# A graph network kernel: in the last message round ScalarE takes a tile's sums first, and two small transfers are issued later in the step

## The reference

```python
def step(h, Wl):                      # five rounds, h is 6250 x 256
    m = h @ Wl
    agg = segment_sum(m[src], dst)    # the neighbours' rows, summed by node
    gi = agg @ w_ih.T + b_ih
    gh = h @ w_hh.T + b_hh
    ...
    r = sigmoid(ir + hr); z = sigmoid(iz + hz)
    ng = tanh(in_ + r * hn)
    return (1 - z) * ng + z * h
...
y = relu(concat([h, x]) @ l0_w.T + l0_b)
y = relu(y @ l1_w.T + l1_b)
```

## Time and profile before

| | us |
|---|---|
| median of 3 runs | 9063.8 (9062.63 to 9071.94) |
| the profiled execution's own time | 9073.26 |
| its span in the trace | 9071.5 |
| PE busy | 6295.3 (69%) |
| POOL busy | 6524.4 (72%) |
| DVE busy | 5542.8 (61%) |
| ACT busy | 2574.8 (28%) |

### The profile page before, as it was taken

One profiled execution on the slowest core, in us unless ns is written; L12 is line 12 of the kernel. 1 busy time (PEld: TensorE's weight loads), 2 busy tenths in 40 slices (PEclk: granted clock), 3 DMA queues, 4 the chain that ended last, 5 costly groups with the idle time before them and its releaser, 6 DMA issues. The chain is left out here.

```text
span 9071.5 us, 161491 instructions
## 1 busy us (share of the span) xinstructions
PE 6295.3 (69%) x36545; PEld 5409.3 (60%) x36546; DVE 5542.8 (61%) x13908; ACT 2574.8 (28%) x6581; POOL 6524.4 (72%) x7005
## 2 busy tenths in 40 slices
PE   0011255552444498888888888888888999889998
PEld 0000133332333377777777677767776888778887
DVE  9999444442444466656665566656664666556666
ACT  4223111112333211121112111111112333456665
POOL 1777777777777777767777677767776777657776
PEclk9755566665555599999999999999999999989999
DMA  4000222222222244434443444444443444212223
GB/s 153 7 7 18 58 79 77 78 68 61 59 59 59 80 143 137 138 103 143 137 138 108 137 139 136 129 117 138 138 138 104 135 124 127 71 53 63 64 64 53
DMA packets 428100, 870.71 MB, mean 96 GB/s; under 512 B 117433, under 2 KB 229680, under 8 KB 427349
## 3 DMA queue, kind: packets, MB, share of 16 engines
q0 software_dynamic: 269952, 615.62, 25.2%
q10 hardware_dynamic: 122250, 189.76, 6.2%
q1 hardware_dynamic: 35529, 61.49, 2.1%
HBM read 763.02 MB, written 103.40 MB: 96 GB/s over the span
## 5 line engine op out<-in xcount | busy, mean ns | idle before, releaser
L1027 POOL DMA_INDIRECT rows<-state_table,rec x3440 | 3290.6, 957 | 1185.9 <-issue 1105.8
L1100 PE MATMUL l_prod<-rows,onehot 128*125 x10728 | 2640.3, 399 | 1210.6 <-SPq L1041 523.8
L1141 DVE TENSOR_TENSOR agg<-agg,l_prod 125x256 f32 (+2 forms) x5364 | 2038.7, 380 | 2185.2 <-PE l_prod L1100 1156.2
L1100 PEld LDWEIGHTS l_prod<-rows,onehot 128*125 128x125 f32 x10728 | 2010.8, 223 | 1637.4 <-issue 1440.4
L2313 POOL DMA_INDIRECT w_area<-xcol_table,l_slots x832 | 787.7, 947 | 346.6 <-issue 250.4
L1027 POOL DMA_INDIRECT rows<-rel_table,rec x782 | 740.4, 947 | 255.5 <-issue 238.2
L1027 POOL DMA_INDIRECT rows<-in_x_dram,rec x782 | 740.8, 947 | 251.2 <-issue 232.0
L1837 PE MATMUL l_prod<-l_sources,rec 125*125 125x256 f32 x3000 | 695.1, 382 | 24.6 <-DMA rec<-dense_table 23.9
L474 POOL DMA_INDIRECT slots_table<-rec_stage,row_stage x528 | 553.1, 1048 | 161.6 <-issue 143.2
L1837 PEld LDWEIGHTS l_prod<-l_sources,rec 125*125 125x125 f32 x3000 | 562.9, 189 | 118.2 <-DMA rec<-dense_table 30.8
L1792 PE MATMUL l_rh<-state,w_area 128*128 x4000 | 591.0, 282 | 3.0 <-DVE l_u L2121 3.0
(11 more groups left out here) (427 smaller groups left out, 10314.1 us busy)
## 6 DMA issues: line engine op xcount, KB each, us to landing
rec<-dense_table ACTq DMA_DIRECT2D x125, 732.4 KB
rows<-state_table,rec POOLq DMA_INDIRECT x3440
l_sources<-state_table ACTq DMA_DIRECT2D x125, 250.0 KB
rel_table<-l_relrow ACTq DMA_DIRECT2D x50, 500.0 KB
state_table<-l_row ACTq DMA_DIRECT2D x200, 125.0 KB
dense_table<-late_rec SPq DMA_DIRECT2D x50, 366.2 KB
w_area<-xcol_table,l_slots POOLq DMA_INDIRECT x832
rows<-in_x_dram,rec POOLq DMA_INDIRECT x782, 2.5
```

Of the source, the lines that this page charges most:

```text
L1027: pool.indirect_dma_start(out=K["rows"][:, r, 0:width], out_offset=None, in_=table, in_offset=bass.IndirectOffsetOnAxis(ap=K["rec"][:, wor ...
L1100: last = pe.matmul(slots[k][0:LANES, 0:width], K["onehot"][:, h % ONEHOTS, k, :], rows[:, bass.ds(at[k], width)], start=True, stop=True)
L1141: dve.tensor_tensor(into, into, of, ALU.add).then_inc(S.added, 1)
```

## The change

Three things move in `last_body`, all on ACT. The load of x, with its wait and register load, goes from ahead of `take` to the end of part n = 1. The store of the projected columns goes from the end of its own step's n = 3 to n = 1 of the next step (so it names `turn.has(b, 3)` and the other buffer). `take` thereby comes first.

```diff
                     load_next(turn, b, LAST)
                     for n in range(4):
                         if n == 0 and now is not None:
-                            if turn.has(b, 2):
-                                act.wait_ge(y_step, turn.place_in_round(b, 2) * 2 + 2)
-                            tile = numbers_of(nc, act, ACTE, K["slot_tile1"], turn.place_in_round(b), 1, TILES - 1)[0]
-                            act.dma_start(xs[:, odd, :], x2_rows[:, bass.ds(tile, 1), :].rearrange("p t f -> p (t f)"))\
-                                .then_inc(xs_in[odd], 16)
                             take(turn, b, now)
...
                             last.then_inc(hid_ok, 1)
+                        if n == 1 and now is not None:
+                            if turn.has(b, 2):
+                                act.wait_ge(y_step, turn.place_in_round(b, 2) * 2 + 2)
+                            tile = numbers_of(nc, act, ACTE, K["slot_tile1"], turn.place_in_round(b), 1, TILES - 1)[0]
+                            act.dma_start(xs[:, odd, :], x2_rows[:, bass.ds(tile, 1), :].rearrange("p t f -> p (t f)"))\
+                                .then_inc(xs_in[odd], 16)
+                        if n == 1 and turn.has(b, 3):
+                            place = turn.place_in_round(b, 3)
+                            tile = numbers_of(nc, act, ACTE, K["slot_tile1"], place, 1, TILES - 1)[0]
+                            act.wait_ge(proj_ok, place + 1)
+                            act.dma_start(col_rows[:, bass.ds(tile, 1), :].rearrange("p t f -> p (t f)"),
+                                          colrow[:, 1 - odd, :]).then_inc(col_out[1 - odd], 16)
...
                             act.copy(K["agg"][0:LANES, bass.ds(old, D)], proj_ps[0:LANES, 0, :]).then_inc(proj_ok, 1)
-                            act.wait_ge(proj_ok, place + 1)
-                            act.dma_start(col_rows[:, bass.ds(tile, 1), :].rearrange("p t f -> p (t f)"),
-                                          colrow[:, odd, :]).then_inc(col_out[odd], 16)
```

More of the change, by code:

```diff
@@ L2072, in last_body @@
                             old = numbers_of(nc, act, ACTE, K["slot_col1"], place, 1, (TILES - 1) * SLOT)[0]
-                            tile = numbers_of(nc, act, ACTE, K["slot_tile1"], place, 1, TILES - 1)[0]
                             act.wait_ge(proj_ps_ok, place + 1)
```

## The result

The changed kernel takes 8968.6 us (8965.9 to 8976.5, 4 runs), the kernel before 9063.2 (9055.8 to 9071.9, 4 runs): a ratio of 0.9899 [0.9886, 0.9912], 94.7 us less. The forecast was 52.5 us less, 9011 us, and its range ended at 8998. The sign was right, and the size a little over half of what came.

A forecast was written before the change was run, and what follows sets the result against it. In the last message round PE was taken to set the pace, waiting for ACT's `take`. Terms of 22.5 + 18 + 12 = 52.5 us gave 9011 us from the median 9063.8, range 8998 to 9036 us.

The forecast's parts named there:

- first part: Last message round: PE sets the pace, waiting 22.5 us for ACT's `take`, once in each of 20 b = 0 steps.
- what is late next: Chunk sum of n = 1 (L1100), behind L1852: moves up with it; 0.2 us a turn, 4 us, left to the range.
- don't hold it: Chunk sum of n = 1: DVE's dense additions end at 7783.30, before PE would come to it at 7784.51.
- Term 1: b = 0 steps of the last round: PE's wait for `take` goes whole, 22.5 us.
- Term 2: Windows from b = 0 to b = 1: eight slow-clock windows recover once PE's wait goes, 18 us, lower bound nothing.
- the gathers become the bound: Turns of the last round: POOL's ring empties in places, half of 40 us is lost, 9031 us; chance 0.10.
- Term 3: Six tail steps: ACT reaches `take` sooner after the last copy, 2.0 of 2.78 us each; 12 us, bounds 9.5 and 15.
- the rival with 0.12: Tail: the clock comes back there too, 7 us more, 9004 us; chance 0.12.
- What it adds: Mid-step on ACT, ahead of gate z: two issues and two loads, 1.9 us, covered by waiting, so costing nothing.
- the sign that it named: ACT's wait before gate z shrinks to about 2 us in the steps and under 1 in the tail, but stays.
- The figure of 50 ns: DMA dispatch time; by it two issues free 0.1 us of ACT, not 1.04, and the tail gives about 6 us.
- x load too late: L1916 of the next step: x landing after about 12.8 us makes a loss, 9126 us at 14 us; chance 0.03.

The follow-up runs named there:

- before_pe_loads_2: Kernel before, ACT untouched; only PE's register loads for the n = 1 chunk sums moved ahead of its wait for `take`: 9004.1 us, ratio 0.9940.
- store_only_2: Kernel before with only the store of the projected columns moved to n = 1 of the next step: 9021.7 us, ratio 0.9953.
- The single edits: Kernel before with only the load of x moved (8998.0 us), and with only the store of the projected columns moved (9021.7 us).
- after_busy_tail: Changed kernel with PE's n = 1 register loads ahead of its wait for `take`, product h_b repeated twice more in the last three turns: 8979.8 us, ratio 0.9900.

## Why the prediction was half of it

**The sentence that failed** is in its first part: "PE waits for `take` at no b = 1 step before the tail", taken from "PE starts L1852 with no idle time in front of it". The engine was not idle, but its sequence was held until `take` ended (7806.42), and the register loads that the next sum needs came only then. The same step closed the question of "what is late next": the pause behind L1852 was said to follow PE's register loads, "and moves up with L1852", at a gain of 0.2 us in 20 steps. It shrank by 0.6 us at b = 0 and 0.8 at b = 1, 25.7 us in all, for which the sum had nothing. What "moves up" is not tied to L1852 but to the end of `take`. before_pe_loads_2 shows this cause by itself. DVE's additions, which "don't hold it" in the prediction, do hold the sum at b = 1 once the loads are out of the way, for 0.47 us.

**Term 1, 22.5 us:** right, the wait is gone. **Term 2, 18 us of clock:** the clock is back at 1.00 throughout the turns, and PE's busy time fell by 17.0 us. The reason given (PE's idling) is shown for the tail. In the turns the reason is incomplete, and that the size came out is partly luck: removing the pause alone does it too, and store_only_2, whose waits are shorter, loses the clock in more windows.

The parts of the turns now add up: 22.5 + 25.7 + 17.0 = 65 us against 63.9. The single edits sum to more than the whole (57.7 + 13.9 = 71.6); both shorten the same wait, so by itself this shows no other bound. The rival "the gathers become the bound" fits: POOL's wait for freed chunks fell from 50.8 us to 2.7 (about 10 were forecast), and 15 of its writes of slots moved from the turns into the tail (35 to 20; the gathers are 581 in both). It took nothing from what was forecast. That POOL is the floor at 765 to 772 us is argued, not shown by a run of its own. For it speaks that four kernels end there whose PE idles between 19 and 36 us; against it, that PE is itself busy 739.9 of the 764.8 us and is put down as waiting for rows for only 1.5.

**Term 3, the tail:** mis-sized, 12 for 23.4. The remaining register load was counted with 0.7 us behind the copy; it costs nothing, since it runs under the table load, and 2.8 us a step go (5.0 to 2.2, 17 in six steps), above even the bound of 2.5. The rest, 6.4 us, is the clock, and the repeated products give the same (11.2 - 4.8): the rival with 0.12 came true in size, 6.4 us where it had 7, with three of the six steps at 1.00.

**What it adds** was right at nothing, and the cover that it counted on (ACT's wait for gate z) was there. Only the sign that it named was wrong: it saw this wait shrink to 2 us and under 1. It did not move, for it is idle time of ACT's engine, and the issues run in ACT's sequence meanwhile. The figure of 50 ns that the prediction takes from the Trainium skill (DMA: Bandwidth & Descriptors, section "Anatomy of one DMA — SWDGE (gpsimd) path") is for DMAs that POOL issues, by the section's own title. ACT's 0.51 and 0.53 us neither confirm nor contradict it. **x load too late:** no. L1916 follows L1852 in every step with no idle time.

**What is the best version?** No kernel tried is measurably faster than the changed one. after_busy_tail has the shortest tail, 4.8 us less, and the same ratio in whole time (0.9900 against 0.9899).

## What to carry to other kernels

Read two timelines for each engine: its work, and its sequence of register loads, waits and issues. If a load or an issue behind a wait feeds the next instruction, the lateness of what is waited for is paid even where the engine shows no idle time; the pause then stands one instruction further on, under another name ("issue", or whoever came last). Before moving work off an engine that is late, try moving the register loads of the waiting engine ahead of its wait: here that alone brought 56 of 95 us. Behind a wait on the engine's own last result was the dearest place for an issue that was tried here: store and wait together cost 1.9 us a step (2.01 against 0.15), while one issue under the table load cost nothing.

## What was not expected of the hardware

- A register load costs ScalarE 0.28 to 1.10 us, and the issue of one of the two small DMAs 0.51 to 0.53, in a sequence that overlaps the engine's own work. The Trainium skill (Perfetto Trace Analysis, section "DVE / Act Engine Instruction (TENSOR_ADD, Activation, etc)") has the sequencer free as soon as an engine instruction is pushed into its wait queue, and its section "Tensor Engine Instruction (MATMUL, LD_WEIGHTS)" draws the same. Where the semaphore is already there the trace agrees (ScalarE's issue at 7830.28 under L2060). Where it is not, the trace differs: TensorE's register operation behind the waiting L1852 starts at 7783.9 and 7806.5, when `take` has ended, and not before, and so it is in all 40 steps of the turns of before.
- TensorE's granted clock fell in PE's idle stretches of the tail and stayed at 2.4 GHz when they were filled with a repeated product (busy_tail), for 11 us of 95. In the turns its falls do not follow the length of one wait: 8 of 20 windows with waits of 1.2 us, 18 of 20 with waits of 0.5.
- The same kernel takes 9.06 ms on some chips and 11.6 to 11.8 ms on others, where PE stands between matmuls without a releaser in the turns, which gather rows, while the tail has the same length. Why is open. A change worth 1.0% reads there as 0.3 to 0.5%.
